# A selective-scan mixer with a quantised gated FFN: 60 gate units spread over 56 slots in eighths, a second gate eviction at a slot's end, 25 output products a slot

## The chip, the cores and the metric

The kernel runs on one core of a Trainium2 chip. The metric is the device time of one execution in microseconds (us); lower is better. Engines are named as in the profile: PE is TensorE (PEld its weight loads), DVE is VectorE, ACT is ScalarE, POOL is GpSimd, SP is SyncE, which here issues every DMA (its rows are marked SPq). PEclk is the granted TensorE clock as a share of full speed.

## The reference

One layer over L = 2048 tokens and H = 1024 channels: layer norm, then a state-space mixer and a feed-forward part with 4-bit weights, which gates it.

```python
xn = layernorm(x)
proj = xn @ W_in.T;  x, gate = proj[..., :2048], proj[..., 2048:]
x = silu(causal_conv4(x))
ts, B, C = split(x @ W_x.T)                 # each RMS-normed; R = 64, N = 16
dt = softplus(ts @ W_dt.T + b_dt);  A = -exp(A_log)
state = state * exp(dt * A) + (dt * x) * B  # over tokens, for 2048 channels x 16 states
y = sum_n(state * C) + x * D
s = (y * silu(gate)) @ W_out.T
g = silu(ffn(xn))   # down(silu(gate(xn)) * up(xn)), I = 2752, 4-bit weights plus low-rank parts
out = x + s * g
```

## The kernel before

A first phase (about 546 us) computes the normed input, the convolved `x`, `dt` and the B and C tables, and stores most of it in HBM. The change touches it only in a few semaphores. The second phase is a loop of SLOTS = 256 **slots**, s = 0 to 255. A slot is one state index n of one step; a step (16 slots) is one chunk of T = 512 tokens (C = 4 chunks) for one group of J = 4 tiles of 128 channels (G = 4 groups). In each slot

- POOL makes the scan's input `inj` (`pool.tensor_tensor`, 128x2048, L1653), some slots ahead, in a ring of four;
- ACT makes four decays (L1377), DVE runs four scans over them (`scan`, L1517);
- PE transposes the scanned tiles of the slot before (`turn`, four groups t = 0 to 3 of four transposes, L1703). DVE adds groups 0 to 2, weighted with C, into `ysum` (`add_up`, L1535), ACT and POOL do group 3 (`weigh` L1415, L1665).

In every fourth slot (n = 3, 7, 11, 15, from slot 19 on) PE transposes a finished `ysum` back (`y_back`, L1714) and DVE adds the D term to it (`d_u`, L1544).

Between a slot's turns PE does dense work in four pieces (`piece(0)` to `piece(3)`), so that one stage follows another:

- **gate stage**, slots 0 to FF0 - 1 = 59: `gate_product`. There are GATES = 64 gate units (16 tiles of 128 gate channels by 4 chunks), four of them done in the first phase (EARLY), so 60 are left, one for each slot. A unit is 8 eighths (h) of three matmuls each (L1726), accumulated in one of three PSUM banks (`bank[u % 3]`). In the next slot ACT takes the tanh (L1435, to the single buffer `ex`) and DVE multiplies (L1569) into `gout[:, u % 2]`, between its second scan and its second `add_up`. SP stores `gout` to `gs_s` (L1244). DVE may write a half of `gout` only when the store of the unit two before has landed (`atleast(v, z_st[u % 2], ...)`).
- **FFN stage**, 88 slots from FF0: `product`, 32 matmuls a slot and `low_rank`; a high and a low fp16 part of each result are stored (`h_s`, L1263) from the double buffer `hh` (ACT's `high`, L1406, waits for the store of two units before).
- **down stage**, 64 slots from DOWN0 = 150.
- **out stage**, from OUT0 = 216: `out_product`, 24 of 1536 matmuls (L1821) a slot, 48 for each of 32 results z. What the 40 slots leave (576 matmuls) runs after the last slot, the **tail**. The last 384 matmuls (z of 24 and more, constant `late`) need the last token chunk's y: PE waits there once for `e_y` (loads of stored y) and `e_lo` (the last DVE result of the chain `d_u`, multiply, subtract, L1544, L1615, L1618/L1621, that follows the four last `y_back`).

Gate weights come in halves of 512 columns: SP loads a half (L1140) into the one buffer `gr` (a name in `work`), ACT scales and rounds it (`gate_high`, L1396, L1399), POOL makes the low part (`gate_low`, L1631), one half every second slot. Tables of slots place the side jobs: `DQ_AT` (22 tiles of the down weights), `WO_AT` (32 halves of the output weights: load, convert on ACT, two stores).

The order of work on each engine is the order in which this loop is written out. SP's queue too is in program order, and a wait at its head holds all that is behind it. In an odd slot SP first waits for `inj` of two slots ahead and loads the next two B rows (`load_bb`, L1136), then comes the store of the gate unit finished two slots before. In slots with n = 2 it loads `dd` for the next step (four DMAs, 2 MB).

## Time and profile before

| | |
|---|---|
| median of three runs | 2763.37 us (2761.09 to 2766.05) |
| the profiled execution's own time | 2765.08 us, span 2763.3 us |
| busy share of the span | PE 96%, DVE 87%, POOL 72%, ACT 57%, PEld 55% |
| 16 DMA engines, HBM | 54.8% of their time, 162 GB/s over the span |
| granted TensorE clock, mean | 0.99 |

Busy time is what an engine's instructions cover, including the waits inside a pipelined PE; it does not say which engine sets the pace in a stage. For that one reads each stage by itself, and in it which engine has no gap before the instruction that starts its next round.

### The profile page before, as it was taken

What the parts mean: (1) busy time and instruction counts of PE and PEld (TensorE: products, weight loads), DVE (VectorE), ACT (ScalarE), POOL (GpSimd) and SP (SyncE); (2) the same over time, 40 slices, a digit from 0 to 9 for tenths busy, and PEclk for the clock granted to TensorE, in tenths of its full rate; (3) what the DMA queues carried; (4) which work ended last, traced back from release to release, by engine and by line L of the source; (5) the groups of instructions that cost most, each with busy time, mean ns of one, the idle gap of its engine ahead of it and who ended that gap; (6) DMA issues with size and microseconds to landing.
All of it is one profiled execution on the core that took longest, in us unless ns stands there. A gap on an engine that the chain in (4) does not pass through costs nothing.

```text
span 2763.3 us, 41632 instructions
## 1 busy us (share of the span) xinstructions
PE 2658.4 (96%) x14980; PEld 1530.1 (55%) x14980; DVE 2402.0 (87%) x2914; ACT 1584.3 (57%) x2643; POOL 1982.7 (72%) x943
## 2 busy tenths in 40 slices
PE   6999999799999999999999999989999998999999
PEld 3545555355555555555555555556666665555644
DVE  5988877699999998888888888899999999999920
ACT  4454645666666667777776776654555555445500
POOL 2311223288999988889897988788889888999811
PEclk9999999999999999999999999999999999999999
DMA  7755477255555545454544444665555658667541
GB/s 250 235 179 193 134 272 205 101 164 193 162 172 174 168 125 166 130 161 123 170 129 142 139 143 132 180 200 117 158 150 127 162 129 243 169 178 190 150 127 57
DMA packets 338797, 449.09 MB, mean 163 GB/s; under 512 B 170592, under 2 KB 181088, under 8 KB 334496
## 3 DMA queue, kind: packets, MB, share of 16 engines
q1 hardware_dynamic: 338592, 446.43, 54.8%
q8 instruction: 120, 1.97, 0.3%
q14 instruction: 85, 0.70, 0.1%
HBM read 312.39 MB, written 133.96 MB: 162 GB/s over the span
## 4 chain that ended last, share of the span: by engine, by line
PE 35%; DVE 28%; issue 11%; POOL 3%; DMA 3%; ACT 1%; DVEq 0%; SPq 0%; POOLq 0%; ACTq 0%
DVE inj L1517 15%; DVE ysum L1535 9%; PE main_bank L1745 6%; PE main_bank L1747 6%; PE xtp_turned L1703 6%; PE main_bank L1821 4%; PE misc_bank L1747 3%; PE misc_bank L1745 3%; PE misc_bank L1821 2%; DMA h_s<-work 2%; POOL inj L1653 2%; DVE work L1569 1%; DMA gs_s<-work 1%; PE main_bank L1756 1%; DVE us L1544 1%
## 5 line engine op out<-in xcount | busy, mean ns | idle before, releaser
L1653 POOL TENSOR_TENSOR inj<-dd,bb 128x2048 f32<-128x2048 f32 x255 | 1156.1, 4534 | 235.3 <-PE xtp_turned L1703 233.5
L1703 PE MATMUL xtp_turned<-ident,inj 128*128 128x128 f32 x4096 | 628.6, 277 | 45.1 <-DVE inj L1517 34.7
L1517 DVE TENSOR_TENSOR_SCAN inj<-ssm_decay,carry,inj 128x512 f32<-128x512 f32 x512 | 656.4, 1282 | 2.5 <-ACT ssm_decay L1377 2.4
L1517 DVE TENSOR_TENSOR_SCAN inj<-main_decay,carry,inj 128x512 f32<-128x512 f32 x512 | 653.6, 1277 | 0.5 <-ACT main_decay L1377 0.3
L1703 PEld LDWEIGHTS xtp_turned<-ident,inj 128*128 128x128 f32 x4096 | 504.4, 142 | 261.2 <-DVE inj L1517 91.7
L1535 DVE SCALAR_TENSOR_TENSOR ysum<-xtp_turned,cT,ysum 128x512 f32<-128x512 f32 x721 | 534.4, 741 | 99.8 <-PE xtp_turned L1703 98.6
L1377 ACT ACTIVATE main_decay<-dd,aneg 128x512 f32<-128x512 f32 x511 | 351.2, 687 | 381.4 <-DVE inj L1517 381.1
L1377 ACT ACTIVATE ssm_decay<-dd,aneg 128x512 f32<-128x512 f32 x511 | 352.6, 690 | 307.7 <-DVE inj L1517 306.3
L1745 PE MATMUL main_bank<-xx,work 128*128 128x512 f16 x936 | 356.8, 381 | 2.5 <-ACT work L1390 2.5
L1747 PE MATMUL main_bank<-xx,work 128*128 128x512 f16 x936 | 356.7, 381 | 0.0
L1665 POOL TENSOR_TENSOR ysum<-ysum,work 128x512 f32<-128x512 f32 x239 | 306.5, 1282 | 10.5 <-ACT work L1415 10.5
L1726 PE MATMUL main_bank<-xx,work 128*128 128x512 f16 x960 | 235.6, 383 | 8.8 <-PEq L278 8.8
L894 PE MATMUL main_bank<-xx,work 128*128 128x512 f16 x1008 | 226.2, 382 | 3.0 <-DMA work<-w_s 3.0
L1415 ACT ACTIVATE work<-xtp_turned,cT 128x512 f32<-128x512 f32 x239 | 162.0, 678 | 44.3 <-PE xtp_turned L1703 24.5
L1821 PE MATMUL main_bank<-xx,work 128*128 128x512 f16 x768 | 185.5, 381 | 0.0
L1747 PE MATMUL misc_bank<-xx,work 128*128 128x512 f16 x472 | 179.6, 381 | 0.0
L1745 PE MATMUL misc_bank<-xx,work 128*128 128x512 f16 x472 | 179.4, 380 | 0.0
L894 PEld LDWEIGHTS main_bank<-xx,work 128*128 128x128 f16 x1008 | 97.5, 99 | 119.0 <-issue 6.7
L821 POOL TENSOR_TENSOR taps<-halo,inj 128x12 f32<-128x12 f32 x36 | 10.0, 304 | 199.4 <-DVE halo L633 199.4
L1726 PEld LDWEIGHTS main_bank<-xx,work 128*128 128x128 f16 x960 | 94.5, 99 | 89.4 <-issue 12.9
L1747 PEld LDWEIGHTS main_bank<-xx,work 128*128 128x128 f16 x936 | 92.0, 98 | 86.3 <-issue 1.4
L1745 PEld LDWEIGHTS main_bank<-xx,work 128*128 128x128 f16 x936 | 92.0, 98 | 86.3 <-ACT work L1390 2.7
(206 smaller groups left out, 3930.3 us busy)
## 6 DMA issues: line engine op xcount, KB each, us to landing
bb<-bt_s SPq DMA_DIRECT2D x128, 512.0 KB, 6.0
work<-w_s SPq DMA_DIRECT2D x48, 512.0 KB, 3.8
work<-in_gu_q SPq DMA_DIRECT2D x88, 256.0 KB, 3.4
h_s<-work SPq DMA_DIRECT2D x88, 256.0 KB, 3.8
u_s<-inj SPq DMA_DIRECT2D x64, 256.0 KB, 4.5
dd<-dt_s SPq DMA_DIRECT2D x32, 512.0 KB, 8.8
gs_s<-work SPq DMA_DIRECT2D x64, 256.0 KB, 6.1
us<-u_s SPq DMA_DIRECT2D x60, 256.0 KB, 5.3
```

Source lines behind the costliest of these rows:

```text
L894: mm = pe.matmul(main[u % 3][:, :], ww[:, u % 3, part, k * P:(k + 1) * P], xx[:, c, side, k, :], start=(k == 0 and part + side == 0), stop ...
L1377: act.activation(decay[j % 2][:, :], dtb[:, step % 2, j, :], ACT.Exp, scale=aneg[:, step % G * J + j, n:n + 1]).then_inc(s_dec, 1)
L1415: act.activation(ysum[:, step % 2, ADDS, :] if n == 0 else ev[:, :], turned[ADDS % 2][:, :], ACT.Copy, scale=cT[:, step // G * TPC + ADDS, ...
L1517: v.tensor_tensor_scan(inj[:, s % RING, j, :], decay[j % 2][:, :], inj[:, s % RING, j, :], carry[:, step % G * J + j, n:n + 1], ALU.mult, ...
L1535: v.scalar_tensor_tensor(dst, turned[t % 2][:, :], weight, dst, ALU.mult, ALU.add).then_inc(s_sum, 1)
L1653: pool.tensor_tensor(inj[:, e % RING, :, :], dub[:, step % 2, :, :], bb[:, e % 8:e % 8 + 1, :].broadcast_to([P, J, T]), ALU.mult).then_inc ...
L1665: pool.tensor_tensor(ysum[:, step % 2, ADDS, :], ysum[:, step % 2, ADDS, :], ev[:, :], ALU.add).then_inc(s_acc, 1)
L1703: mm = pe.transpose(turned[t % 2][:, j * P:(j + 1) * P], inj[:, s % RING, j, t * P:(t + 1) * P], ident[:, :])
L1726: mm = pe.matmul(bank[u % 3][:, :], gw[w % 2][:, part, h * P:(h + 1) * P], xx[:, c, side, h, :], start=(h == 0 and part + side == 0), stop ...
L1745: pe.matmul(dst[:, :], w, xx[:, p, 0, h, :], start=(h == 0), stop=False, skip_group_check=True)
L1747: mm = pe.matmul(dst[:, :], w, xx[:, p, 1, h, :], start=False, stop=False, skip_group_check=True)
L1821: mm = pe.matmul(bank[z % 3][:, :], y, (wo_hi, wo_hi, wo_lo)[w][:, i, half * T:(half + 1) * T], start=(i == 0 and w == 0), stop=(i == DT - ...
```

## The change

`FF0` goes from 60 to 56. The 60 gate units (480 eighths) are spread over 56 slots: slot s takes eighths 480s/56 to 480(s+1)/56, rounded down (`gate_cut`), 8 in 24 slots and 9 in 32. Four slots finish two units (13, 27, 41 and 55; `gates_done`); the slot after then evicts both, the first at the old place, the second at its end (`gate_tanh` after `weigh` on ACT, `gate` after the fourth scan on DVE). The FFN, down and out stages start four slots earlier, so the out stage has 44 slots, with `OUT_MS` = 25 matmuls in each; 436 instead of 576 matmuls are left for the tail. `DQ_AT` is closer set, `WO_AT` moves with `FF0`. The halves of the gate weights alternate between `gr` and `gr_next`, each with a semaphore (`z_in[0]`, `z_in[1]`), come in slots given by `GATE_HALF_AT`, and a load waits for the low part of the half two before, not one before.

```diff
-FF0 = GATES - EARLY
+FF0 = GATES - 2 * EARLY
...
-DQ_AT = tuple(7 * i // 3 for i in range(IT))
+DQ_AT = tuple(9 * i // 4 for i in range(IT))
+GATE_HALF_AT = {max(1, (2 * h - 7) * FF0 // (GATES - EARLY)): h for h in range(EARLY, 2 * DT)}
+OUT_MS = 25
...
+            def gate_cut(s):
+
+                return tuple((GATES - EARLY) * HK * r // FF0 for r in (s, s + 1))
+
+            def gates_done(s):
+
+                if not 0 <= s < FF0:
+                    return (EARLY - 1,) if s == -1 else ()
+                a, b = gate_cut(s)
+                return tuple(EARLY + m // HK for m in range(a, b) if m % HK == HK - 1)
+
             def out_cut(s):
 
-                return 24 * (s - OUT0), 24 * (s - OUT0 + 1)
+                return OUT_MS * (s - OUT0), OUT_MS * (s - OUT0 + 1)
...
-                    def load_gate(half, dst):
-                        sp.dma_start(dst, win[DT + half // 2, :, half % 2 * T:(half % 2 + 1) * T]).then_inc(z_in, 16)
+                    def load_gate(half):
+                        sp.wait_ge(z_lo, LEAD + half - 1)
+                        sp.dma_start((gr, gr_next)[half % 2][:, :], win[DT + half // 2, :, half % 2 * T:(half % 2 + 1) * T]
+                                     ).then_inc(z_in[half % 2], 16)
...
-                        half = (s + EARLY) // 2 + 2
-                        if s % 2 == 0 and half < 2 * DT:
-                            sp.wait_ge(z_lo, LEAD + half)
-                            load_gate(half, gr[:, :])
-                        u = s - 2 + EARLY
-                        if EARLY - 1 <= u < GATES:
+                        if s == 0:
+                            load_gate(EARLY)
+                        if s + 1 in GATE_HALF_AT:
+                            half = GATE_HALF_AT[s + 1]
+                            if half > EARLY:
+                                load_gate(half)
+                        for u in gates_done(s - 2):
                             w, c = divmod(u, C)
                             sp.wait_ge(z_g, LEAD + u + 1)
                             sp.dma_start(gs_s[w // J, c, :, w % J, :], gout[:, u % 2, :]).then_inc(z_st[u % 2], 16)
...
+                    def gate(u):
+                        v.wait_ge(z_ex, LEAD + u + 1)
+                        atleast(v, z_st[u % 2], u // 2 * 16)
+                        v.scalar_tensor_tensor(gout[:, u % 2, :], ex[:, :], 1.0, bank[u % 3][:, :],
+                                               ALU.add, ALU.mult).then_inc(z_g, 1)
+
...
+                        for u in gates_done(s - 1)[:1]:
+                            gate(u)
...
                         scan(s, 3)
+                        for u in gates_done(s - 1)[1:]:
+                            gate(u)
...
                             if s < FF0:
-                                gate_product(s + EARLY, 2 * u, 2 * u + 2)
+                                a, b = gate_cut(s)
+                                for m in range(a + (b - a) * u // 4, a + (b - a) * (u + 1) // 4):
+                                    gate_product(EARLY + m // HK, m % HK, m % HK + 1)
```

**DVE, slots 14 and 15.** From the gate eviction of slot 14 to that of slot 15, before (L1569 is `gate`, L1517 a scan, L1535 `add_up`, `z_st0` and `z_st1` the landed stores of even and odd units):

```order
L1569 SCALAR_TENSOR_TENSOR work<-work,misc1_bank2 128x512 [waits z_st1,z_ex]
L1535 SCALAR_TENSOR_TENSOR ysum<-xtp1_turned1,cT,ysum 128x512 [waits s_sum,s_turn]
L1517 SCALAR_TENSOR_TENSOR inj<-main0_decay0,carry,inj 128x512 [waits s_dec]
L1535 SCALAR_TENSOR_TENSOR ysum<-xtp0_turned0,cT,ysum 128x512 [waits s_sum,s_turn]
L1517 SCALAR_TENSOR_TENSOR inj<-ssm_decay1,carry,inj 128x512 [waits s_dec]
L1517 SCALAR_TENSOR_TENSOR inj<-main0_decay0,carry,inj 128x512 [waits s_dec,s_inj]
L1535 SCALAR_TENSOR_TENSOR ysum<-xtp0_turned0,cT,ysum 128x512 [waits s_sum,s_turn]
L1517 SCALAR_TENSOR_TENSOR inj<-ssm_decay1,carry,inj 128x512 [waits s_dec]
L1569 SCALAR_TENSOR_TENSOR work<-work,main1_bank0 128x512 [waits z_st0,z_ex]
```

and in the changed kernel (L1572 is `gate`, L1538 a scan, L1556 `add_up`):

```order
L1572 SCALAR_TENSOR_TENSOR work<-work,misc1_bank2 128x512 [waits z_st1,z_ex]
L1556 SCALAR_TENSOR_TENSOR ysum<-xtp1_turned1,cT,ysum 128x512 [waits s_sum,s_turn]
L1538 SCALAR_TENSOR_TENSOR inj<-main0_decay0,carry,inj 128x512 [waits s_dec]
L1556 SCALAR_TENSOR_TENSOR ysum<-xtp0_turned0,cT,ysum 128x512 [waits s_sum,s_turn]
L1538 SCALAR_TENSOR_TENSOR inj<-ssm_decay1,carry,inj 128x512 [waits s_dec]
L1572 SCALAR_TENSOR_TENSOR work<-work,main1_bank0 128x512 [waits z_st0,z_ex]
L1538 SCALAR_TENSOR_TENSOR inj<-main0_decay0,carry,inj 128x512 [waits s_dec,s_inj]
L1556 SCALAR_TENSOR_TENSOR ysum<-xtp0_turned0,cT,ysum 128x512 [waits s_sum,s_turn]
L1538 SCALAR_TENSOR_TENSOR inj<-ssm_decay1,carry,inj 128x512 [waits s_dec]
L1572 SCALAR_TENSOR_TENSOR work<-work,main2_bank1 128x512 [waits z_st1,z_ex]
```

Units 17, 18 and 19 are evicted within these rows, where before 17 and 18 were: 18 stands at slot 14's end, and 19, which writes the same half of `gout` as 17 and so waits for `z_st1`, follows one slot after 17 and not two.

**SP, slots 13 to 15.** Before (L1136 is `load_bb`, L1140 a half of the gate weights, L1244 a gate unit's store, L1248 and L1252 the down weights' store and load):

```order
L1136 DMA bb<-bt_s 128x2x512 [waits s_inj]
L1244 DMA gs_s<-work 128x512 [waits z_g]
L1248 DMA dw_s<-work 128x1024 [waits q_cv]
L1140 DMA work<-in_win 128x512 [waits z_lo]
L1244 DMA gs_s<-work 128x512 [waits z_g]
L1252 DMA work<-in_dq 128x1024 [waits q_cv]
L1136 DMA bb<-bt_s 128x2x512 [waits s_inj]
L1244 DMA gs_s<-work 128x512 [waits z_g]
```

and in the changed kernel (L1150, L1155, L1261, L1265 and L1269 in the same roles):

```order
L1150 DMA bb<-bt_s 128x2x512 [waits s_inj]
L1155 DMA work<-in_win 128x512 [waits z_lo]
L1261 DMA gs_s<-work 128x512 [waits z_g]
L1265 DMA dw_s<-work 128x1024 [waits q_cv]
L1269 DMA work<-in_dq 128x1024 [waits q_cv]
L1155 DMA work<-in_win 128x512 [waits z_lo]
L1261 DMA gs_s<-work 128x512 [waits z_g]
L1150 DMA bb<-bt_s 128x2x512 [waits s_inj]
L1261 DMA gs_s<-work 128x512 [waits z_g] x2
```

The stores of units 17 and 18 stand together, behind slot 15's `load_bb`; in slot 13 a load of gate weights now stands ahead of the store, where before the store came first.

**PE, from the last `y_back` on.** Before (L1714 is `y_back`, L1821 `out_product`):

```order
L1714 MATMUL misc0_back<-ident,ysum 128x128 [waits s_yev]
L1714 MATMUL misc0_back<-ident,ysum 128x128 x3
L1821 MATMUL main1_bank0<-xx,work 128x512 [waits o_r]
L1821 MATMUL main1_bank0<-xx,work 128x512 x47
L1821 MATMUL main2_bank1<-xx,work 128x512 [waits o_y1,o_r]
L1821 MATMUL main2_bank1<-xx,work 128x512 x47
L1821 MATMUL misc1_bank2<-xx,work 128x512 [waits o_r]
L1821 MATMUL misc1_bank2<-xx,work 128x512 x47
L1821 MATMUL main1_bank0<-xx,bb 128x512 [waits o_r,e_lo,e_y]
```

and in the changed kernel, from the last `y_back` but one (L1739 and L1846):

```order
L1739 MATMUL misc0_back<-ident,ysum 128x128 [waits s_yev]
L1739 MATMUL misc0_back<-ident,ysum 128x128 x3
L1846 MATMUL misc1_bank2<-xx,work 128x512 x12
L1739 MATMUL misc0_back<-ident,ysum 128x128 [waits s_yev]
L1739 MATMUL misc0_back<-ident,ysum 128x128 x3
L1846 MATMUL misc1_bank2<-xx,work 128x512 x4
L1846 MATMUL main1_bank0<-xx,bb 128x512 [waits o_r,e_lo,e_y]
```

Between the last `y_back` and the wait for `e_lo` and `e_y` stand 4 matmuls, where 144 stood.

## Rows read from the trace of the kernel before

**Rows 1.** Busy by stage (gate, FFN, out, tail): PE, PEld, DVE, ACT, POOL, PEclk, DMA

```profile
546.50:993.80 447.30, 432.19 (x2432) 253.15 (x2431) 442.50 (x488) 298.36 (x512) 403.23 (x168) 0.99 0.54 167
993.80:1832.50 838.70, 821.43 (x4519) 472.83 (x4517) 731.77 (x830) 594.24 (x1064) 723.40 (x361) 0.99 0.51 148
...
2340.10:2629.60 289.50, 285.55 (x1637) 171.83 (x1636) 285.93 (x310) 143.44 (x250) 268.13 (x121) 0.99 0.64 180
2629.60:2763.30 133.70, 128.68 (x610) 59.96 (x608) 19.99 (x30) 3.15 (x5) 21.21 (x17) 1.00 0.28 85
```

**Rows 2.** Timeline, DVE, one gate slot: start, us, line; then ACT's `weigh`

```profile
709.96 1.27 DVE L1517 TENSOR_TENSOR_SCAN inj<-main_decay,carry,inj 128x512 f32<-128x512 f32 x1
712.97 0.68 DVE L1569 SCALAR_TENSOR_TENSOR work<-work,main_bank 128x512 f32<-128x512 f32 x1
717.23 1.27 DVE L1517 TENSOR_TENSOR_SCAN inj<-main_decay,carry,inj 128x512 f32<-128x512 f32 x1
...
708.89 0.67 ACT L1415 ACTIVATE work<-xtp_turned,cT 128x512 f32<-128x512 f32 x1
```

**Rows 3.** Timeline, PE, the same slot: a turn, six products, a turn

```profile
711.90 0.60 PE L1703 MATMUL xtp_turned<-ident,inj 128*128 128x128 f32 x4
712.34 1.46 PE L1726 MATMUL misc_bank<-xx,work 128*128 128x512 f16 x6
713.63 0.60 PE L1703 MATMUL xtp_turned<-ident,inj 128*128 128x128 f32 x4
```

**Rows 4.** Timeline, POOL and SP, slots 8 to 10 of the gate stage

```profile
613.29 4.54 POOL L1653 TENSOR_TENSOR inj<-dd,bb 128x2048 f32<-128x2048 f32 x1 [1.51 <-PE xtp_turned L1703]
...
617.86 0.38 SPq L1136 DMA_DIRECT2D bb<-bt_s  x1
618.28 0.47 SPq L1244 DMA_DIRECT2D gs_s<-work  x1
...
620.59 0.91 SPq L1244 DMA_DIRECT2D gs_s<-work  x1
```

**Rows 5.** DVE around slot 10's gate; chain; view of the store's line

```profile
621.74 1.28 DVE L1517 TENSOR_TENSOR_SCAN inj<-main_decay,carry,inj 128x512 f32<-128x512 f32 x1
...
625.02 0.69 DVE L1569 SCALAR_TENSOR_TENSOR work<-work,main_bank 128x512 f32<-128x512 f32 x1 [0.17 <-DMA gs_s<-work]
...
618.28 6.64 DMA gs_s<-work
...
  DVE work L1569: 2.8, 4
...
DMA to landing us min/median/max: 3.2/6.1/7.6
```

**Rows 6.** FFN stage, slot 116: chain, then ACT's timeline

```profile
1505.67 8.38 DMA h_s<-work
...
1514.14 0.63 ACT L1406 ACTIVATE work<-work 128x512 f16<-128x512 f32 x1 [4.44 <-DMA h_s<-work]
```

**Rows 7.** Out stage: busy in slots 232 to 235; ACT's wait; DVE's timeline

```profile
2455.50:2486.80 31.30, 28.75 (x165) 17.07 (x164) 28.78 (x32) 14.28 (x26) 31.30 (x16) 1.00 0.52 143
...
ACT work L1415 <- POOL ysum L1665: 11.0, 6, 3.7
...
2486.20 0.72 DVE L1544 SCALAR_TENSOR_TENSOR us<-us,dsk,misc_back 128x512 f32<-128x512 f32 x1
2486.84 1.28 DVE L1517 TENSOR_TENSOR_SCAN inj<-main_decay,carry,inj 128x512 f32<-128x512 f32 x1
```

**Rows 8.** Busy in two stretches behind the stall of Rows 6, columns as Rows 1

```profile
1515.30:1518.30 3.00, 1.74 (x9) 1.04 (x10) 2.41 (x3) 2.97 (x7) 2.53 (x3) 0.91 0.00 0
1518.30:1521.30 3.00, 3.00 (x11) 1.66 (x10) 3.00 (x5) 2.70 (x5) 1.51 (x2) 0.52 0.45 132
```

**Rows 9.** Timeline of the tail, and the last y load's landing

```profile
2637.57 0.32 SPq L1356 DMA_DIRECT2D dd<-y_s  x1
2644.13 0.60 PE L1714 MATMUL misc_back<-ident,ysum 128*128 128x128 f32 x4
2644.57 20.88 PE L1821 MATMUL main_bank<-xx,work 128*128 128x512 f16 x96
2647.00 0.69 DVE L1621 TENSOR_TENSOR dd<-dd 128x512 f16<-128x512 f32 x1
...
dd<-y_s SPq DMA_DIRECT2D x1, 1024.0 KB, 5.8
```

More of the change, by code:

```diff
@@ L372, in _ @@
                             for half in range(2):
[L373 removed]
+                                sp.dma_start(gout[:, half, :], win[DT, :, half * T:(half + 1) * T]).then_inc(z_in[half], 16)
                         if u >= 2:
@@ L1634, in _ @@
                     for e in range(SLOTS + 6):
-                        half, odd = divmod(e + EARLY, 2)
-                        if odd == 0 and EARLY <= half < 2 * DT:
-                            gate_low(half, gr[:, :])
+                        if e - 3 in GATE_HALF_AT:
+                            half = GATE_HALF_AT[e - 3]
+                            gate_low(half, (gr, gr_next)[half % 2][:, :])
                         if e - 4 in WO_AT:
```

61 lines of the change are left out of this document (29 added, 32 removed).

## The prediction, written before the changed kernel had run

> **What bounds the kernel now.** I read the page first, for the shape, then the busy time of each stage, then one slot's timeline on DVE and on PE, then SP's queue and where its stores land, last the chain. The page's shares (PE 96%, DVE 87%) are means over stages with different limits, so they decide nothing.
>
> In the gate stage [rows 1] 60 slots take 447.3 us, 7.46 each. An ordinary slot is 7.27 from scan to scan, and DVE has no gap in it [rows 2]. PE needs for one turn and six products 1.73 [rows 3]: a matmul 0.216, a turn of four transposes 0.43. A slot of 24 matmuls is 4 x 0.43 + 24 x 0.216 = 6.92, so PE waits 0.35 for DVE. **The gate stage is DVE's, by 0.35 us a slot.** The FFN stage (34 matmuls a slot: 9.06, with `y_back` 9.17, of the measured 838.7 / 88 = 9.53) is PE's. In the out stage a DVE slot with a result is like one with an eviction, 7.27, one without is 0.6 shorter, and `d_u` adds 0.64 (2486.20 to 2486.84 [rows 7]): four slots with two results come to 2 x 7.27 + 2 x 6.67 + 0.64 = 28.5, 7.13 each; PE's to 6.92 + 0.11 for the `y_back`, 7.03. Measured are 289.5 / 40 = 7.24 [rows 1], because slots 232 to 235 took 31.3 with POOL busy for all of them and ACT waiting on POOL [rows 7]. The tail is PE's alone, 129 of 134 us [rows 1].
>
> The second thing to see is a thin margin. In slot 9 (start 614.47) SP gets past `load_bb` at 617.86, once the inject that POOL began at 613.29 is done, and issues the odd store at 618.28 [rows 4], 3.8 into the slot. It lands after 6.64, and DVE's `gate` of slot 10, which wants that half of `gout`, starts at 625.02, 3.28 into slot 10 and not 3.01 as elsewhere [rows 2, 5]. So a store has 7.27 + 3.01 - 3.81 = 6.47 us, and needs 6.1 in the median. Before, this cost DVE 2.8 us in all, in 4 waits [rows 5].
>
> **The change, part by part.** The sum is made against the profiled execution, 2765.1 us.
>
> 1. *Four gate slots go.* 4 x 447.3 / 60 = -29.8, but their four evictions stay. -30 with the longer `y_back` slot among them.
> 2. *Second evictions*, slots 14, 28, 42 (that of slot 56 lies under PE). An eviction takes DVE 0.6 (0.68 in [rows 2], less the overlap with what follows). ACT ends `weigh` 0.4 before the next scan round is due (708.89 + 0.67 against 709.96) and must then do a tanh of 0.57, so DVE waits 0.15. 3 x 0.75 = +2.3.
> 3. *The third unit after a double.* Units 17, 18, 19 are evicted in slots 14 (middle), 14 (end) and 15 (middle). 19 overwrites 17. SP issues the store of 17 only behind slot 15's `load_bb`, which waits for the inject of slot 17. That ends as in slot 9, 3.38 into an ordinary slot, 0.75 less because slot 14 is longer: the store goes out 3.38 - 0.75 + 0.42 = 3.05 into slot 15 and lands 6.3 later (between the median 6.1 and the 6.64 of rows 5) at 9.35. DVE stands at 3.01. It waits **6.3 us**, with `add_up`, two scans and PE's fourth turn queued behind. The same in slots 29 and 43 (the doubles 13, 27, 41 all put the store into an odd SP slot): 3 x 6.3 = **+19**. Bounds from rows 5: landing after 3.2, +9.7; after 7.6, +23; nothing, if SP were past `load_bb` earlier, which rows 4 exclude unless POOL runs a slot further ahead.
> 4. *PE in nine-eighth slots*: 27 matmuls, 7.56, against DVE's 7.27. One such slot between two of eight is made good (0.35 idle against 0.29 excess); two in a row leave about 0.3, eight times, half of them beside a `y_back` slot that absorbs most: +1.3. *Gate loads ahead of odd stores*: in 14 odd slots SP now issues a gate half between `load_bb` and the store: 0.42 later and 256 KB more in front. Against the 6.47 allowed that is a wait of some 0.6 in slots up to 13 (six times) and 0.1 later, where `y_back` has moved the rhythm. +3.7. Together +5; bounds 0 (the loads fit in) and +12 (every landing at 7.3).
> 5. *Entry to the FFN*, last eviction and last two stores late: +0.8. Bounds 0 and 3.
> 6. *FFN stage.* In slot 116 a store of `h_s` took 8.38 behind the `dd` loads and ACT waited 4.44 [rows 6]. By the tables this needs a `WO_AT` store in a slot with n = 2 and a `WO_AT` load in the next. Before: slots 114 and 130; after, with `WO_AT` four slots earlier and n = 2 unmoved: 66 and 82. Two each. Of the weaker sort (store in the slot behind) one becomes two, at about 1.5: +1.5. Bounds 0 and +4. At the stage borders `dd` loads now fall on the down and out weights: +0.5, bounds 0 and +5 (PE had slack before the first out product).
> 7. *Out stage*, 44 slots. With 25 matmuls PE needs 4 x (1.73 + 5.40) + 0.44 = 28.96 for four slots, more than DVE's 28.5: **PE becomes the pace**, 7.24. 44 x 7.24 = 318.6; the first slots run at the low clock, +1.3; POOL's knot at 232 to 235 stays, for its load grows with the results, but the slots are longer: +2.5 of the 2.8 before. 322.4 - 289.5 = **+33**. Were DVE still the pace it would be 44 x 7.13 + 2.5, +27.
> 8. *Tail*: 140 matmuls fewer, -30.2. But the cover of the last chain is gone. After the last `y_back` (2644.13) PE had 144 matmuls; DVE's last subtract ends at 2647.69 [rows 9]. With four matmuls PE is at the wait at 2644.57 + 0.87 = 2645.44: +2.3. The last y load went out at 2637.57 and took 5.8, done at 2643.4, so it isn't the one waited for, by 2 us. An idle PE may lose clock, +0.8. -27.1.
>
> Sum: -30 + 2.3 + 19 + 5 + 0.8 + 1.5 + 0.5 + 33 - 27.1 = **+5.0**, 2770.1 for a profiled execution. That one lay 1.7 above the median of the runs, so **2768.4** for the median. The gain of the reordering is about 14 us, and one buffer's reuse eats it.
>
> **The clock in the stalls.** PE stands for some 5 us in each stall of part 3. Behind the 4.44 us stall of slot 116 the granted clock was 0.91 and then 0.52 in two stretches of 3 us [rows 8], the lower level, 1.2 GHz. What is left of PE's slot then (a turn and six or nine products, 1.7 to 2.4 at full clock) takes up to twice that, while DVE itself has 3.0 to go: at most 1 us late, 0 to +3 in all. I take 0, inside the range. The Trainium skill ("TensorE: Matmul & The Clock Gate", Part 1) says that an idle array falls to half clock; by it the sum would be at the upper end of this, 2771; the trace agrees on the fall.
>
> **Rivals.**
> - *The store is no wait* (POOL or SP is further ahead): part 3 is 0, the sum -14, 2749. Against it: SP's order in the change, and rows 4.
> - *The stores land fast*, in 3.2 as the fastest did: part 3 is +9.7, part 4's loads cost nothing (+1.3), the sum -8, 2755. Against it: median 6.1, and slot 10 waited. The Trainium skill ("DMA: Bandwidth & Descriptors", Anatomy of one DMA) gives about 2.0 us plus bytes over 436 GB/s, fitted to transfers that GpSimd issues, an estimate of 2.6 us for 256 KB; by it part 3 would be 8 us and the sum about -10, 2754. The trace shows 6.1, with a 512 KB load issued 0.4 before.
> - *PE does not become the pace in the out stage* and POOL's knot stays: +27 instead of +33, 2762.
> - *Slower*: every store behind a gate load or beside more traffic lands at 7.3, near the largest of rows 5. Part 4 is +12, part 3 +22: the sum +15, **2778**. It decides for slower from a landing of about 6.4 on (then the sum passes +5.5). For it: gate loads, two stores at once and the closer `DQ_AT` share SP's odd slot. Against it: a DMA issued later did not delay earlier ones before.
>
> **How the numbers follow.** A measurement here tells 0.2%, 5.5 us, from no change. Forecast 0.47 (own range 2762 to 2774), no wait 0.12, fast landings 0.08, DVE still the pace 0.13, slow landings 0.20. The forecast lies just under the bound, so it is split 0.24 same, 0.22 slower, 0.01 faster. Faster: 0.12 + 0.08 + 0.01 + a little of the third = 0.22; slower: 0.20 + 0.22 = 0.42; same: the rest, 0.36. The range takes in 2751 to 2779, from the fast landings to the slow ones.
>
> **What would show it.** DVE idle before `gate` in slots 15, 29 and 43, about 6 us each, ended by the landing of `gs_s`, with PE idle beside it; idle of under 1 us before `gate` in slots 4 to 14. DVE waiting on PE's turns in the out stage, 7.24 a slot. PE idle for 2.3 us in the tail, ended by DVE's subtract, and some 30 us less of `out_product` there. Two `h_s` waits of over 4 us, at slots 68 and 84. Wrong would be: no wait in slot 15 (part 3), or `e_y` later than `e_lo` (part 8).

## The result and the profile after

The changed kernel takes 2776.01 us (median of 5 runs, 2773.63 to 2777.94), the kernel before 2763.37 beside it (5 runs): ratio 1.0045, 95% interval 1.0034 to 1.0056. It is 12.6 us slower. The forecast was 2768.4 in 2751 to 2779, with slower, at 0.42, as the likeliest of the three outcomes. The profiled execution has a span of 2774.2, against 2763.3 before.

First the busy time by stage of the changed kernel (gate, out, tail), with the columns of [rows 1]:

```profile
546.80:998.70 451.90, 425.64 (x2358) 248.77 (x2357) 416.78 (x460) 284.08 (x486) 375.65 (x156) 0.97 0.52 161
...
2343.50:2667.50 324.00, 321.06 (x1841) 194.46 (x1840) 315.89 (x341) 157.21 (x274) 299.37 (x135) 0.99 0.64 181
2667.50:2774.20 106.70, 99.51 (x475) 46.58 (x472) 18.87 (x28) 3.81 (x7) 17.44 (x14) 1.00 0.26 90
```

The gate stage is the odd one. It has four slots fewer and is 4.5 us longer (451.8 from its first scan to that of slot 56, against 447.3 in [rows 1]); DVE has 26 us less work than before and is idle for 35 us, where it was idle for 5. Measured from first scan to first scan, the whole difference of the spans is:

| stretch | before | after | difference | forecast |
|---|---|---|---|---|
| gate stage | 447.3 | 451.8 | +4.5 | -3.7 |
| FFN stage (88 slots) | 823.0 | 822.2 | -0.8 | +2.3 with the entry |
| down stage | 523.3 | 522.7 | -0.6 | +0.5, both borders |
| out stage up to slot 255 (39, 43 slots) | 282.2 | 316.7 | +34.5 | +33 |
| slot 255 and tail | 141.0 | 114.0 | -27.0 | -27.1 |

With 0.3 in front of the first slot this is 10.9 us, the difference of the spans. The forecast missed the stage that it had thought about most.

The view of the gate store's line (L1261) says who waits for it and how long it takes to land, where [rows 5] had 4 waits:

```profile
  DVE work L1572: 29.1, 12
...
DMA to landing us min/median/max: 2.5/6.6/8.7
```

The timeline around slot 15 (663.21 to 676.66; start, duration, engine, line; chosen rows). Slot 14 evicts its second unit at 662.6; SP can store neither unit of the double before `load_bb`, whose wait ends with POOL's inject:

```profile
661.03 4.53 POOL L1678 TENSOR_TENSOR inj<-dd,bb 128x2048 f32<-128x2048 f32 x1 [0.70 <-PE xtp_turned L1728]
662.61 0.69 DVE L1572 SCALAR_TENSOR_TENSOR work<-work,main_bank 128x512 f32<-128x512 f32 x1
665.59 0.38 SPq L1150 DMA_DIRECT2D bb<-bt_s  x1
666.31 0.80 SPq L1261 DMA_DIRECT2D gs_s<-work  x2
672.37 0.69 DVE L1572 SCALAR_TENSOR_TENSOR work<-work,main_bank 128x512 f32<-128x512 f32 x1 [6.05 <-DMA gs_s<-work]
673.78 1.12 PE L1728 MATMUL xtp_turned<-ident,inj 128*128 128x128 f32 x4 [5.84 <-DVE ysum L1556]
674.68 2.77 PE L1751 MATMUL misc_bank<-xx,work 128*128 128x512 f16 x6
678.57 1.46 PE L1751 MATMUL main_bank<-xx,work 128*128 128x512 f16 x6
```

The store goes out 3.10 us into slot 15 (forecast: 3.05) and DVE stands for 6.05 (forecast: 6.3). Then something that I had priced at nothing: six products behind the pause take PE 2.77 us instead of 1.46. The busy time in four stretches from the stall on (the last three columns are PEclk, DMA, GB/s) says why:

```profile
660.00:672.00 12.00, 7.66 (x43) 4.16 (x41) 6.18 (x7) 6.26 (x11) 7.25 (x4) 0.95 0.42 117
673.00:676.00 3.00, 2.22 (x8) 1.34 (x9) 3.00 (x5) 0.99 (x2) 1.02 (x1) 0.50 0.55 215
676.00:680.00 4.00, 4.00 (x19) 2.03 (x18) 3.15 (x4) 2.33 (x5) 4.00 (x2) 0.79 0.02 4
680.00:684.00 4.00, 4.00 (x27) 2.52 (x26) 4.00 (x6) 2.40 (x4) 0.73 (x1) 1.00 0.00 0
```

PE resumes at 0.50, the lower level of 1.2 GHz, and is back at full clock at 680. Slot 16 is 8.23 us long and not 7.27; slots 30 and 44, behind the other two stalls, 8.93 and 8.36. In slot 29 (775.91 to 791.28) the store also has a half of the gate weights in front of it, and goes out 4.24 into the slot:

```profile
779.22 0.37 SPq L1150 DMA_DIRECT2D bb<-bt_s  x1
779.64 0.47 SPq L1155 DMA_DIRECT2D work<-in_win  x1
780.15 1.25 SPq L1261 DMA_DIRECT2D gs_s<-work  x2
```

That slot is 15.38 long, slot 15 13.45 and slot 43 13.55. The chain that ended last has the DMA of `gs_s` in it eleven times; here the two of slots 15 and 17 (start, us):

```profile
666.31 5.96 DMA gs_s<-work
...
689.00 6.81 DMA gs_s<-work
```

In the FFN stage the long `h_s` store of [rows 6] stands where it was forecast, in slots 68 and 84 (11.64 and 12.26 us); a third, in slot 116 (11.12, ACT waits 4.18), was not forecast. The first one in the chain:

```profile
1104.13 8.65 DMA h_s<-work
```

and in ACT's timeline:

```profile
1112.86 0.63 ACT L1428 ACTIVATE work<-work 128x512 f16<-128x512 f32 x1 [4.70 <-DMA h_s<-work]
```

The out stage: the busy time of four of its slots (compare the slots of [rows 7]), then of the last microseconds before the stage and the first in it:

```profile
2401.90:2430.90 29.00, 29.00 (x171) 17.71 (x170) 28.84 (x32) 14.41 (x25) 28.40 (x14) 1.00 0.67 191
...
2340.00:2343.50 3.50, 0.80 (x7) 0.51 (x5) 3.50 (x4) 1.78 (x3) 3.08 (x1) 0.99 1.05 390
2343.50:2350.00 6.50, 5.36 (x16) 2.33 (x15) 4.57 (x6) 1.72 (x4) 3.88 (x3) 0.50 1.05 386
```

and PE's timeline over the border:

```profile
2343.03 0.80 PE L1728 MATMUL xtp_turned<-ident,inj 128*128 128x128 f32 x4 [2.70 <-DVE inj L1538]
2344.97 1.44 PE L1846 MATMUL main_bank<-xx,work 128*128 128x512 f16 x3 [1.14 <-DMA xx<-wo_s]
```

PE is busy for all 29.00 us of the four slots, so it is the pace, at 7.25 a slot. The stage's first slot takes 9.55, against 7.20 before: the first products wait for the `wo_s` weights in a DMA that is full (its share is 1.05, at 386 GB/s), and PE then works at half clock.

The tail, in PE's and DVE's timeline from the last `y_back` but one on (which [rows 9] has at 2644.13):

```profile
2682.92 0.60 PE L1739 MATMUL misc_back<-ident,ysum 128*128 128x128 f32 x4
2683.36 1.03 PE L1846 MATMUL misc_bank<-xx,work 128*128 128x512 f16 x4
2685.80 0.69 DVE L1646 TENSOR_TENSOR dd<-dd 128x512 f16<-128x512 f32 x1
2686.59 5.34 PE L1846 MATMUL main_bank<-xx,bb 128*128 128x512 f16 x24 [2.21 <-issue]
```

and the busy time behind it:

```profile
2686.50:2692.50 6.00, 5.91 (x28) 2.75 (x29) 1.19 (x2) 0.00 (x0) 2.49 (x2) 1.00 0.51 162
```

Four products, then an idle 2.21 us (forecast: 2.3). The profile names no releaser for it, but PE starts 0.10 after the end of DVE's last subtract (2685.80 + 0.69); the last load of y had landed at 2681.29, so it was not what PE waited for. The clock behind it is 1.00.

### The profile page after: what moved, and what is told of

Read it like the earlier page. It is cut to its first block, busy times and chain, and to the rows that moved or that the text cites. A ratio compares the mean times of both kernels' runs of the same rounds, so it can differ in the third digit from the quotient of the medians.

```text
span 2774.2 us, 41634 instructions
## 1 busy us (share of the span) xinstructions
PE 2656.2 (96%) x14980; PEld 1535.0 (55%) x14980; DVE 2408.3 (87%) x2914; ACT 1584.1 (57%) x2643; POOL 1982.8 (71%) x943
## 4 chain that ended last, share of the span: by engine, by line
PE 45%; DVE 18%; issue 7%; DMA 5%; POOL 4%; ACT 1%; SPq 1%; DVEq 0%; POOLq 0%; ACTq 0%
DVE inj L1538 9%; PE xtp_turned L1728 9%; PE main_bank L1846 7%; PE main_bank L1770 7%; PE main_bank L1772 7%; DVE ysum L1556 6%; PE misc_bank L1772 3%; PE misc_bank L1770 3%; POOL inj L1678 3%; PE misc_bank L1846 3%; DMA gs_s<-work 3%; PE main_bank L1751 2%; DMA h_s<-work 2%; PE misc_bank L1751 1%; PE main_bank L1781 1%
## 5 line engine op out<-in xcount | busy, mean ns | idle before, releaser
L1728 PE MATMUL xtp_turned<-ident,inj 128*128 128x128 f32 x4096 | 628.0, 277 | 54.3 <-DVE inj L1538 29.1
L1538 DVE TENSOR_TENSOR_SCAN inj<-ssm_decay,carry,inj 128x512 f32<-128x512 f32 x512 | 653.8, 1277 | 2.6 <-ACT ssm_decay L1394 2.6
L1538 DVE TENSOR_TENSOR_SCAN inj<-main_decay,carry,inj 128x512 f32<-128x512 f32 x512 | 651.0, 1272 | 0.6 <-ACT main_decay L1394 0.3
L1556 DVE SCALAR_TENSOR_TENSOR ysum<-xtp_turned,cT,ysum 128x512 f32<-128x512 f32 x721 | 531.1, 737 | 107.0 <-PE xtp_turned L1728 105.9
L1846 PE MATMUL main_bank<-xx,work 128*128 128x512 f16 x768 | 189.3, 382 | 1.1 <-DMA xx<-wo_s 1.1
```

Source lines behind the costliest of these rows:

```text
L1538: v.tensor_tensor_scan(inj[:, s % RING, j, :], decay[j % 2][:, :], inj[:, s % RING, j, :], carry[:, step % G * J + j, n:n + 1], ALU.mult, ...
L1556: v.scalar_tensor_tensor(dst, turned[t % 2][:, :], weight, dst, ALU.mult, ALU.add).then_inc(s_sum, 1)
L1728: mm = pe.transpose(turned[t % 2][:, j * P:(j + 1) * P], inj[:, s % RING, j, t * P:(t + 1) * P], ident[:, :])
L1846: mm = pe.matmul(bank[z % 3][:, :], y, (wo_hi, wo_hi, wo_lo)[w][:, i, half * T:(half + 1) * T], start=(i == 0 and w == 0), stop=(i == DT - ...
```

## The experiments

Medians in us; each ratio is to the kernel before, run beside it on the same chip. Besides the table, times of stages are from the profiled executions. Two kernels with the same gate stage tell how far those repeat: 451.8 us in the changed kernel and 452.6 in e4, 417.7 in e7 and 418.7 in e10.

| kernel | median | ratio, 95% interval |
|---|---|---|
| changed kernel | 2776.0 | 1.0045 [1.0034, 1.0056] |
| e1_store_first | 2744.7 | 0.9926 [0.9914, 0.9939] |
| e2_doubles_shift | 2761.2 | 0.9990 [0.9981, 0.9998] |
| e3_load_behind | 2774.0 | 1.0033 [1.0020, 1.0045] |
| e4_out24 | 2779.7 | 1.0048 [1.0034, 1.0062] |
| e5_before_store_first | 2761.0 | 0.9992 [0.9983, 1.0002] |
| e6_before_out25 | 2758.6 | 0.9978 [0.9970, 0.9987] |
| e7_load_store_bb | 2744.1 | 0.9926 [0.9914, 0.9938] |
| e8_three_first | 2753.9 | 0.9963 [0.9949, 0.9976] |
| e9_evict_together | 2748.9 | 0.9946 [0.9932, 0.9959] |
| e10_dt_later | 2753.1 | 0.9962 [0.9950, 0.9975] |

**e1_store_first.** The stores ahead of both loads:

```diff
+                        for u in gates_done(s - 2):
+                            w, c = divmod(u, C)
+                            sp.wait_ge(z_g, LEAD + u + 1)
+                            sp.dma_start(gs_s[w // J, c, :, w % J, :], gout[:, u % 2, :]).then_inc(z_st[u % 2], 16)
                         if s % 2 == 1 or s == 0:
                             pair = (s + 9) // 2
...
-                        for u in gates_done(s - 2):
-                            w, c = divmod(u, C)
-                            sp.wait_ge(z_g, LEAD + u + 1)
-                            sp.dma_start(gs_s[w // J, c, :, w % J, :], gout[:, u % 2, :]).then_inc(z_st[u % 2], 16)
```

> SyncE issues the stores of finished gate units ahead of the load of the next bb pair in its slot; nothing else differs from the changed kernel. Theory (the stores queued behind the bb load are the whole of what the stage lost): the trace of the changed kernel shows 29.1 us in which the gate eviction waits for a gs_s store to land, 12 times; they vanish. Slots 15, 29 and 43 fall from 13.5, 15.4 and 13.6 us to about 7.5, and the slots behind them (8.2, 8.9, 8.4) to 7.6: about 28 us less, 2748 us, which would be some 15 under the kernel before. Rival (the stall only hides TensorE, which cannot do 60/56 of the matmuls in a slot of 7.5 us): the waits vanish but the plain slots grow, 10 us less at most, 2766. Second rival (the bb load, now later, is awaited by the first additions of a slot in its turn): slots 14, 28 and 42 grow by what 15, 29 and 43 lose, 2770 to 2776.

2744.7 us, 31 less than the changed kernel. The gate stage of this kernel:

```profile
548.40:968.40 420.00, 416.74 (x2358) 246.32 (x2357) 415.11 (x458) 283.57 (x486) 375.70 (x156) 0.99 0.56 173
```

In the view of the store's line nobody stands under the heading of those who waited:

```profile
who waited for it (us, times):
...
DMA to landing us min/median/max: 2.4/5.8/10.1
```

The median over all stores (5.8 against 6.6, and up to 10.1) says little of the three that had been waited for. For the double before slot 15 (slot 15 starts at 660.66 here), SP and DVE in the timeline (chosen rows), then the landing of the first store alone:

```profile
656.21 4.89 SPq L1250 DMA_DIRECT2D gs_s<-work  x2
663.69 0.66 DVE L1572 SCALAR_TENSOR_TENSOR work<-work,main_bank 128x512 f32<-128x512 f32 x1
...
DMA to landing us min/median/max: 3.0/3.0/3.0
```

The store goes out 4.45 us before the slot's start, where in the changed kernel it went out 3.10 behind it, and with no `bb` load issued just ahead of it lands after 3.0 us and not 5.96. In slots 29 and 43 the landings are 3.8 and 4.8 us, against 6.75 and 6.41. The earlier issue would have been enough by itself: DVE wants the buffer 7.5 to 7.6 us after the issue in all three cases, more than any of the landings in the changed kernel's stalls. The shorter landing comes on top, and no run separates the two. Slots 15, 29 and 43 take 7.29, 7.29 and 7.93. Both rivals fall: plain slots of 60/56 of the products stay at 7.27, and the later `bb` load is awaited by no one. The gate stage has 420.0 us against 451.8, which is all of the gain (31.8 us there, 31.3 in the medians).

**e2_doubles_shift.** The doubles in slots 14, 28 and 42, stored in even slots:

```diff
-                return tuple((GATES - EARLY) * HK * r // FF0 for r in (s, s + 1))
+                return tuple((GATES - EARLY) * HK if r == FF0 else max(0, ((GATES - EARLY) * HK * r - 28) // FF0)
+                             for r in (s, s + 1))
```

> The cut of the gate products is 28/56 of an eighth later, so that the units of a double are finished in slots 14, 28 and 42 instead of 13, 27 and 41, evicted in 15, 29 and 43, and stored in SyncE's even slots, where no bb load stands ahead of the stores. SyncE's order within a slot is as in the changed kernel. Theory (the bb load ahead of the store makes the stall, not the double): the three stalls of 6 to 8 us go, with the long slot behind each, 20 to 24 us less; the shorter waits of plain odd slots (2, 6, 10, 34, 38 at 8.2 to 10.1 us) stay: 2753 us. Rival (two evictions in one slot, or three units in two slots over two buffers, stall by themselves): the stalls only move one slot on, within 3 us of the changed kernel's 2776.

2761.2, 15 less and not 23. Slot 15 falls to 9.75, but slot 29 has 11.61 and slot 43 10.05. DVE and SP in slot 29 (it starts at 772.93):

```profile
776.55 0.37 SPq L1151 DMA_DIRECT2D bb<-bt_s  x1
...
777.48 0.43 SPq L1262 DMA_DIRECT2D gs_s<-work  x1
...
783.94 0.69 DVE L1573 SCALAR_TENSOR_TENSOR work<-work,main_bank 128x512 f32<-128x512 f32 x1 [3.65 <-DMA gs_s<-work]
```

The first store in this slot is that of slot 28's unit, again behind `bb`; the double's second unit wants its buffer at the slot's end, where it used to be wanted a slot later. I had overlooked this user. So neither theory was whole: the `bb` load makes the wait, and the double decides who is hit.

**e3_load_behind.** The order `bb` load, stores, gate load.

```diff
-                        if s + 1 in GATE_HALF_AT:
-                            half = GATE_HALF_AT[s + 1]
-                            if half > EARLY:
-                                load_gate(half)
                         for u in gates_done(s - 2):
...
+                        if s + 1 in GATE_HALF_AT:
+                            half = GATE_HALF_AT[s + 1]
+                            if half > EARLY:
+                                load_gate(half)
```

> The load of a gate half (256 KB from HBM) is issued behind the gate stores of its slot instead of ahead of them; the bb load stays ahead. Theory (each gate load ahead of a store makes the store later by its own issue and its share of the transfer, about 0.5 to 2 us): slot 29, the one double with a gate load ahead of its stores, falls from 15.4 to about 13.5, and the even slots behind a gate load (2, 6, 10, 18, 34, 38) fall by 0.5 to 0.8 each: 5 us less in all, 2771 us. Rival (the bb load alone holds the stores): under 1.5 us less, 2775. Rival (the halves now come late for ScalarE's conversion and TensorE waits): 2778 or more.

2774.0, 2 less; with the spreads of both this is little more than the runs can tell. The profiled execution says more: its gate stage is 4.3 us shorter (447.5), which is more than the repeats differ by, while its tail happens to be 1.7 longer. Slot 29 falls from 15.38 to 14.25, slot 43 grows from 13.55 to 14.41, the sum of all waits falls from 29.1 to 25.1 us. Outside the three stalls and the slots behind them 2.8 us are gained, in slots 2, 6, 10, 34 and 38 above all (0.5 to 1.1 each, as the theory said; 18 and 46 got longer). So the gate loads' place in SP's queue is not what makes the stalls, and makes a part of the plain waits.

The halves of the gate weights delay these stores by a second way, which this run left as it was. `GATE_HALF_AT` puts 15 of the 27 halves into odd slots of SP's queue, where none were, and `gate_low` on POOL (L1631 before, L1656 after) now often stands right ahead of the inject that `load_bb` waits for. POOL and SP up to the store of slot 37, before (the slot starts at 822.09; `gate_low` stood one inject earlier, at a pause of 0.82):

```profile
811.45 1.15 POOL L1631 TENSOR_TENSOR work<-work 128x512 f16<-128x512 f32 x1
813.42 4.53 POOL L1653 TENSOR_TENSOR inj<-dd,bb 128x2048 f32<-128x2048 f32 x1 [0.82 <-PE xtp_turned L1703]
...
819.12 1.29 POOL L1679 TENSOR_TENSOR gs<-us,gs 128x512 f32<-128x512 f32 x1
820.35 4.55 POOL L1653 TENSOR_TENSOR inj<-dd,bb 128x2048 f32<-128x2048 f32 x1
```

and in the changed kernel (start 846.67):

```profile
843.45 1.28 POOL L1704 TENSOR_TENSOR gs<-us,gs 128x512 f32<-128x512 f32 x1
844.67 1.17 POOL L1656 TENSOR_TENSOR work<-work 128x512 f16<-128x512 f32 x1
845.79 4.55 POOL L1678 TENSOR_TENSOR inj<-dd,bb 128x2048 f32<-128x2048 f32 x1
...
850.36 0.37 SPq L1150 DMA_DIRECT2D bb<-bt_s  x1
850.78 0.47 SPq L1155 DMA_DIRECT2D work<-in_win  x1
851.30 1.35 SPq L1261 DMA_DIRECT2D gs_s<-work  x2
```

The inject ends 3.67 into the slot and not 2.81, the store goes out at 4.63 and not 3.25. In slots 33 and 41 it is the same (injects 3.79 and 3.92, not 2.79 and 2.82); in slots 5 and 9 the inject is 0.30 and 0.0 later and the gate load's 0.5 us is most or all of the delay.

**e4_out24.** `OUT_MS = 24` in the changed kernel.

> 24 output products a slot instead of 25, with the 44 slots of the output stage as in the changed kernel, so 44 products more in the tail; the gate stage is as in the changed kernel. Theory (TensorE sets the length of the output slots with 25 products): the 43 slots fall from 316.7 us to the length that they have in the kernel before (282.2 us over 39, 7.24 each: 311.1), 5.6 us less; the tail grows by 44 products of (141.0 - 114.0)/140 = 0.193 us, 8.5 us: 2779 us. Rival (VectorE sets it, the 25th product is hidden): slots as they are, 2784.5. Rival (a product in a slot costs a full product's 0.216 us): slots 9.3 us less, 2775.

2779.7, as the theory said, with other parts: the 43 slots take 313.0 (3.7 less), four of them 28.6, and slot 255 with the tail 120.3 (6.3 more). In the tail 44 products cost 0.143 us each and not 0.216: the first of them fill the 2.21 us in which PE is idle there (this kernel's trace has no such gap). That is two thirds of the 3.2 us that are missing from 44 x 0.216; the rest was not traced.

**e5_before_store_first.** The move of e1 in the kernel before.

```diff
+                        u = s - 2 + EARLY
+                        if EARLY - 1 <= u < GATES:
+                            w, c = divmod(u, C)
+                            sp.wait_ge(z_g, LEAD + u + 1)
+                            sp.dma_start(gs_s[w // J, c, :, w % J, :], gout[:, u % 2, :]).then_inc(z_st[u % 2], 16)
                         if s % 2 == 1 or s == 0:
```

> The kernel before (60 gate slots, 24 output products) with the stores of finished gate units ahead of the bb load and the gate load, and nothing of the change. Theory (the order matters only once a slot finishes two units): its trace shows 2.8 us of waits for gs_s stores and a few slots that are longer by 0.3 to 2.1 us (2, 10, 14, 30); the gate stage goes from 447.3 to about 444.5 us, the kernel to 2760 to 2762 us, so the other kernel with the stores first (2744.7) keeps some 16 us that belong to the change. Rival (the gain of 31 us is the order's alone and the change itself is worth nothing): 2745 to 2750 us.

2761.0; the gate stage goes from 447.3 to 444.9. The interval of the ratio includes 1. Between this kernel and e1 lies the change alone: 16.3 us less with the stores in front (16.9 against e7, which ran beside this one), where with the stores behind the loads it is 12.6 us more.

**e6_before_out25.** In the kernel before, 25 products a slot and nothing else:

```diff
-                return 24 * (s - OUT0), 24 * (s - OUT0 + 1)
+                return 25 * (s - OUT0), 25 * (s - OUT0 + 1)
...
-                            cuts = tuple(out_cut(s)[0] + 6 * u for u in range(5))
+                            cuts = tuple(out_cut(s)[0] + 25 * u // 4 for u in range(5))
...
-                    first = 24 * (SLOTS - OUT0)
+                    first = 25 * (SLOTS - OUT0)
```

> The kernel before with 25 output products a slot in its 40 output slots, nothing else; 40 products fewer remain for the tail. Theory (in a slot the 25th product costs what separates the four-slot cycles of the traces, 29.02 - 28.56 us, 0.115 a slot; in the tail it costs 0.216): 39 x 0.115 = 4.5 us more and 40 x 0.2156 = 8.6 us less, 2761 us, 0.1% faster than before. Rival (TensorE pays the full 0.216 in the slot as well): no change, 2765. Rival (the tail has nothing left to cover the waits of its last chunk): 2767.

2758.6, a gain of 0.22%: the 39 slots grow by 3.1 us (0.08 each), slot 255 with the tail shrinks by 7.8 (of 8.6 expected). With 25 products PE is the pace; yet the 25th costs only a third of its 0.216. With 24, four slots take 28.55 us (slots 240 to 243 of the kernel before) where PE's own work comes to 28.12, and DVE is busy for all of the 130.00 us from 2490 to 2620: part of the 25th product's time is time in which PE waited for DVE.

**e7_load_store_bb.** Gate load, stores, `bb` load: e1 with the gate load in front. The `bb` load is moved from the head of these lines to their end:

```diff
                         for u in gates_done(s - 2):
...
+                        if s % 2 == 1 or s == 0:
+                            pair = (s + 9) // 2
+                            if pair < STEPS * N // 2:
+                                sp.wait_ge(s_inj, LEAD + 2 * pair - 6)
+                                load_bb(pair)
```

> The changed kernel with the order gate load, stores of gate units, bb load (the changed kernel has bb load, gate load, stores; the one with the stores first has 2744.7 us). Theory (it is the bb load, which waits on SyncE for an injection of the slot, that holds the stores; a gate load ahead costs only its issue): within 3 us of 2744.7, 2746 us. Rival (a gate load ahead of a store slows its landing as much as a bb load does): slot 29 stays above 11 us, 2752 us or more.

2744.1, the same as e1. A gate load ahead of the stores costs nothing as long as SP does not wait for POOL there. The gate stage:

```profile
547.30:965.00 417.70, 415.60 (x2358) 246.54 (x2357) 414.86 (x459) 283.52 (x486) 375.49 (x156) 0.99 0.57 174
```

**e8_three_first.** The stores in front only in the slots behind a double:

```diff
+                        double = len(gates_done(s - 2)) == 2
+                        if double:
+                            for u in gates_done(s - 2):
+                                w, c = divmod(u, C)
+                                sp.wait_ge(z_g, LEAD + u + 1)
...
-                        for u in gates_done(s - 2):
+                        if not double:
+                            for u in gates_done(s - 2):
```

> The changed kernel with the stores ahead of the bb load in the slots behind a double alone (15, 29, 43); all other stores stay behind the bb and gate loads. Theory (three stalls and the slot behind each: 6.2 + 8.1 + 6.3 us over a plain slot, and 1.0 + 1.7 + 1.1 us): 24.4 us less than 2776.0, 2751.6 us; the remaining 7 us to the kernel with all stores first lie in the plain slots 2, 6, 10, 12, 18, 32, 34, 38 and 46. Rival (a stall only moves on: the unit after the next waits instead): slots 16 to 18, 30 to 32 and 44 to 46 grow and less than 15 us is gained, 2761 or more.

2753.9, 22 less. Slots 15, 29 and 43 are at 7.29, 7.29 and 7.93, the slots behind them at 7.27 to 7.29; nothing moves on. Left are 9.5 us of waits in 8 places (slots 2, 6, 10, 18, 34 and 38, and at the first eviction of slots 14 and 42), and to e7 11.2 us of gate stage.

**e9_evict_together.** On e7, both evictions of a double in the middle of the slot:

```diff
-                        for u in gates_done(s - 1)[:1]:
+                        for u in gates_done(s - 1):
...
-                        for u in gates_done(s - 1)[1:]:
-                            gate(u)
```

(ScalarE's tanh moves in the same way.)

> On the kernel with gate load, gate stores, bb load in this order (2744.1 us): the second gate eviction of slots 14, 28, 42 and 56 stands right behind the first on ScalarE and VectorE, not at the slot's end. Theory (the place at the slot's end keeps a distance to the store of the buffer's last unit): VectorE waits in each of the four slots, because the unit two before was evicted a slot earlier and its store, issued 2.7 us later behind a bb load, lands 5.4 us after its issue, that is some 4 us into the slot; 1 to 2 us a double over what the slots have now (8.4, 8.2, 8.2), 2748 us. Rival (the place does not matter): 2744 us, within 1.5. Rival (one switch of work less in the slot): 2742 or less.

2748.9, 4.8 more than e7. Slot 14 on DVE:

```profile
651.43 0.66 DVE L1570 SCALAR_TENSOR_TENSOR work<-work,misc_bank 128x512 f32<-128x512 f32 x1
654.56 0.69 DVE L1570 SCALAR_TENSOR_TENSOR work<-work,main_bank 128x512 f32<-128x512 f32 x1 [2.47 <-DMA gs_s<-work]
```

The mechanism is the expected one, but only slot 14 shows it in full (10.71 us against 8.44); slots 28 and 42 grow by 0.5 and 0.7, slot 42 with a wait of 0.90 for the store and slot 28 with one of 0.72 for ACT. The place at the slot's end is worth having: of the 4.8 us, 3.6 stand in the gate stage.

**e10_dt_later.** On e7, the `dt` loads three slots later, an attempt on the `h_s` waits (the last three lines stood in the block of slot 2 and now stand under the new condition):

```diff
+                        if n == 5 and step + 1 < STEPS:
+                            nc_, ng = divmod(step + 1, G)
+                            b = (step + 1) % 2
                             for half in range(2):
                                 js = slice(half * 2, half * 2 + 2)
                                 sp.dma_start(dtb[:, b, js, :], dt_s[ng, nc_, :, js, :]).then_inc(s_dt[b], 16)
```

> On the kernel with gate load, gate stores, bb load in this order (2744.1 us): the two dt loads of the next step (512 KB each) go to SyncE's slot 5 of the step instead of slot 2, where the two du loads stay. Theory (the waits of ScalarE for h_s stores, 42.9 us in 31 places, longest 5.3, stand where all four loads run ahead of the store's landing; slots 68, 69, 84 have 11.5, 10.9 and 12.3 us against 8.9 to 9.1): the waits fall by half and the FFN stage with them, from 824.1 to about 816 us, the kernel to 2736. Rival (the store waits for the bb load's transfers, which stand in every second slot): the same waits, 2744, or new ones three slots later, up to 2750.

2753.1, a miss: 9 more than e7. The waits for `h_s` and a new one of POOL, in the view of all waits (us in total, times, longest):

```profile
ACT work L1431 <- DMA h_s<-work: 43.1, 41, 3.8
POOL dd L1688 <- DMA dd<-dt_s: 38.2, 12, 4.7
```

Slot 68 is cured (8.88), but slot 70 has 11.79: the wait went two slots on with the traffic, and twelve times, once a step, POOL waits for `dt` itself (in slot 70 for 3.4 us, 6.2 us into the slot). In the profiled executions the FFN stage gains 3.0 us, and the gate, down and out stages lose 1.0, 2.5 and 4.4. At the entry to the out stage the move helps: slot 212, its first, takes 8.34 us and not 9.58, and PE's wait of 1.33 for `wo_s` is gone; later slots of the stage lose more than that.

## Why the prediction was right or wrong, step by step

The forecast was a sum of +5.0 for the profiled execution; it is +10.9. The 1.7 us by which that execution was to lie above the median are the rest of the 7.6 between 2768.4 and 2776.0: this time the profiled execution is the median one. The mechanism that it named holds, a stall at one buffer's reuse; the sign of the gate stage as a whole (+4.5, not -3.7) and that of term 6 do not. Term by term:

1. *Four gate slots go*, -30: -29.7, by e5 (444.9 us for all 60, 415.2 up to slot 56). Right.
2. *Second evictions*, +2.3: +3.0, from slots 14, 28 and 42 in e7 (8.44, 8.24, 8.17, each against 7.27).
3. *The third unit after a double*, +19: slots 15, 29 and 43 are longer by 6.2, 8.1 and 5.6 than with the stores in front (7.29, 7.29, 7.93), 19.9. The time of issue, the landing (5.96, 6.75 and 6.41, where 6.3 was set), the engines queued behind: as written. Right, though in slot 43 the store went out earlier (2.1 into the slot) and in slot 29 later (4.2) than the one figure for all three.
4. *The clock in the stalls*, taken as 0 with a bound of 3: slots 16, 30 and 44 are longer by 1.0, 1.7 and 1.1, **3.7 us**, with no wait for a store in them. The rows after the change show why the step failed. It let what is left of PE's work lie under DVE's 3.0 us; but when PE resumes, DVE resumes too, and DVE needs PE's turns, each of which now stands behind six products at half clock. The row has 2.77 for them. The rule of the Trainium skill that the prediction set beside this ("TensorE: Matmul & The Clock Gate", Part 1: an idle array falls to half clock) was the better guide here: this trace shows 0.50 behind a pause of 5.84 us.
5. *PE in nine-eighth slots and gate loads ahead of odd stores*, together +5: **this is the step that failed**. PE's part is nothing: e7 reaches slot 56 in 417.7 us, and e5 plus the 3.0 of the evictions is 418.2. The waits outside the three stalls, all for stores behind `bb`, are worth 11.2 us (e8 against e7), of which the kernel before had 2.4 (e5): +8.8 where the prediction had 3.7. The reason given, the gate loads issued ahead of the stores, is worth 2.8 of that (e3), a little under its price. What was left out is POOL: `gate_low`, which came along with the halves into the odd slots, stands ahead of the inject that `load_bb` waits for, and in slots 33, 37 and 41 moves it by 0.9 to 1.1 us, in front of the waits of 1.0, 1.0 and 1.4 us in slots 34, 38 and 42. The prediction looked at SP's queue and not at the queue that SP waits for.
6. *Entry, FFN stage, borders*, +2.8: -1.4 (-0.8 and -0.6). Two strong `h_s` waits came in slots 68 and 84 as said (4.70 and 5.32), but with a third of 4.18 in slot 116: the rule by the tables missed it. Others got weaker (the waits for `h_s` are 34.5 us in all, before 35.7): slots 141 and 142 took 12.48 and 10.10 before, the same places of the stage, now slots 137 and 138, take 9.98 and 9.54. Why those did was not tried.
7. *Out stage*, +33: +34.5 over one slot less. PE is the pace at 7.25, as said. The first slot is 2.35 us longer than before; 1.3 was set for its clock, and the late weights (the four `dd` loads of slot 210 stand in the same stretch as the eight of `wo_s`) had been put at 0.5 in term 6. That the two of `dt` among these loads make them late is shown by e10, which issues them three slots later: 1.24 us of the slot go (against e7), and with them PE's wait for `wo_s`. The rest of the 2.35 was not taken apart.
8. *Tail*, -27.1: -27.0, with the idle 2.21 us forecast as 2.3. The 0.8 for lost clock did not come: the granted clock behind it was 1.00.

The gate stage is then -29.7 + 3.0 - 0.5 + 19.9 + 3.7 + 8.8 = +5.2, to be set against the measured +4.5 (e8 and the changed kernel differ by 22.9 there, not by 23.6, hence the 0.7). Terms 4 and 5 are most of what is missing from the forecast, 3.7 and 3.3 us. In the other direction the FFN and down stages came out 4.2 us better than forecast, for reasons not shown; without that luck the result would have been about 2780 us, above the range.

Of the rivals, "no wait" (2749) is what the kernel would have been with the stores in front (2744.1), so that the sum without the stall was about right. "DVE still the pace" fell: the out stage has PE's 7.25 us a slot. "Fast landings" fell: the median rose from 6.1 to 6.6, and the estimate of 2.6 us from the Trainium skill ("DMA: Bandwidth & Descriptors", Anatomy of one DMA) fits none of the changed kernel's stores in the loop but the three issued at the end of a stall (2.5, 2.5 and 2.8). In e1, where many go out with no `bb` load just ahead, several land after 2.4 to 3.0 us, so the traces agree with the estimate for such stores alone. "Slow landings" at 7.3, put at 2778 and nearest to the result by its number, was right in part: the stores that were waited for landed after 5.96 to 6.93 us, none as late as 7.3, and part 3 came out at the forecast's price and not at this rival's. What grew was the lateness of the issue in plain slots. It also said that slower follows from a landing of 6.4 on, and the median was 6.6.

What stays open: how much of the 8.8 us `gate_low`'s place on POOL makes. The trace shows it ahead of the inject, but no run moved it alone. The waits vanish with the stores in front (e1, e7), so they are of stores behind `bb`. The half clock was not tested by itself either; its 3.7 us contain the products' backlog as well.

**The version that beats both kernels** is the change with the stores ahead of the `bb` load: 2744.1 us (e7) or 2744.7 (e1), 0.74% under the kernel before. The change was worth having; it lacked the reordering of one queue.

## What to carry to other kernels

When a change lets a ring of two buffers take two results in a slot, look up what stands ahead of the release of the first one in its queue: the release here was a store behind a load that waits for another engine, and 6.5 us of slack that sufficed for one result a slot did not suffice for two. Look also at the queue of the engine that this load waits for: a side job moved ahead of its work there delays the store as well. Put the stores that free a buffer ahead of loads that wait, and re-price the change after that, not before: the same edit was +12.6 us with one order and -16.3 with the other. After a stall of several microseconds add the half-clock restart of TensorE to the price, if another engine waits for its first results.
